# Feed-forward of an int4 layer: VectorE's down units moved to units 0, 4, 16 and 20, GpSimd's products and ScalarE's conversions re-placed

## The reference

```python
H = 1024; I = 3584; G = 128
Wg, Wu, Wd = (q.reshape(O, In // G, G) * s[:, :, None] for each of gate, up, down)   # q: int32 in [-8, 7]
xn = _layernorm(x)
gate_score = silu(xn @ Wg.T)
intermediate = gate_score * (xn @ Wu.T)
x = x + attention(xn) + intermediate @ Wd.T
```

## Time and profile before

| | |
|---|---|
| median of 3 runs | 2119.39 us |
| the profiled execution: its own time, its span | 2121.04 us, 2119.1 us |
| granted TensorE clock, mean | 0.993 |
| busy: PE, DVE, ACT, POOL | 95%, 75%, 59%, 64% |
| feed-forward | from about 855 us to the end |
| one tile of its loop | 42.79 us |

### The profile page before, as it was taken

How to read it: one execution, slowest core, us unless ns; L and a number is a source line. 1 busy time by engine, 2 the same in 40 slices (tenths; PEclk the granted TensorE clock), 3 DMA queues, 4 the chain that set the end, 5 groups by cost and what they waited for, 6 DMA issues and landing times. The chain is left out here.

```text
span 2119.1 us, 36938 instructions
## 1 busy us (share of the span) xinstructions
PE 2021.6 (95%) x10880; PEld 973.3 (46%) x10880; DVE 1589.2 (75%) x1584; ACT 1253.2 (59%) x2017; POOL 1348.6 (64%) x769
## 2 busy tenths in 40 slices
PE   7899999999998899989999999999999999999997
PEld 5555555555554444334444444444444444444444
DVE  5666766766765310399989998999899989999896
ACT  4577777777776321236565656565666566656653
POOL 1444554554554000048888888888888888888886
PEclk9999999999999999999999999999999999999998
DMA  8464454454455334122211221222112212222108
GB/s 284 94 130 89 94 125 98 89 124 104 89 116 141 112 112 173 30 53 67 59 47 47 69 59 45 49 69 59 45 49 69 57 47 49 54 64 55 49 21 322
DMA packets 330007, 185.97 MB, mean 88 GB/s; under 512 B 269169, under 2 KB 306033, under 8 KB 329969
## 3 DMA queue, kind: packets, MB, share of 16 engines
q1 hardware_dynamic: 329968, 185.46, 33.8%
HBM read 96.29 MB, written 25.17 MB: 57 GB/s over the span
## 5 line engine op out<-in xcount | busy, mean ns | idle before, releaser
L644 PE MATMUL banks<-xt,lower 128*128 128x512 f16 x3584 | 861.7, 379 | 29.8 <-ACT lower L895 16.1
L1212 POOL TENSOR_TENSOR acc<-acc,lower 128x1024 f32<-128x1024 f32 x327 | 771.5, 2364 | 176.4 <-ACT lower L922 176.3
L922 ACT ACTIVATE lower<-banks,down_scale 128x512 f32<-128x512 f32 x654 | 413.1, 682 | 356.6 <-PE banks L669 265.3
L1099 DVE SCALAR_TENSOR_TENSOR lower<-banks,gate_scale,lower 128x1024 f32<-128x1024 f32 x392 | 479.2, 1278 | 146.2 <-PE banks L644 140.3
L644 PEld LDWEIGHTS banks<-xt,lower 128*128 128x128 f16 x3584 | 337.3, 98 | 486.6 <-DVE lower L1099 80.3
L499 PE MATMUL banks<-wt,xt_tile 128*128 128x512 f16 x2304 | 542.0, 380 | 4.2 <-ACT wt L743 2.6
L1099 DVE SCALAR_TENSOR_TENSOR lower<-banks,up_scale,lower 128x1024 f32<-128x1024 f32 x392 | 479.5, 1278 | 50.9 <-PE banks L644 44.8
L669 PE MATMUL banks<-lower 128*128 (+1 forms) x1792 | 459.7, 381 | 4.6 <-DMA lower<-lower 4.4
L1174 POOL TENSOR_TENSOR stacks<-unit,stacks 128x512 f16<-128x512 f32 x192 | 246.9, 1306 | 303.7 <-ACT stacks L768 303.7
L499 PEld LDWEIGHTS banks<-wt,xt_tile 128*128 (+1 forms) x2304 | 215.2, 98 | 216.7 <-issue 4.2
L669 PEld LDWEIGHTS banks<-lower 128*128 (+1 forms) x1792 | 175.6, 98 | 217.7 <-issue 18.3
(11 more groups left out here) (57 smaller groups left out, 1320.3 us busy)
## 6 DMA issues: line engine op xcount, KB each, us to landing
lower<-in_L_ffn_gate_q_dram SPq DMA_DIRECT2D x28, 512.0 KB, 3.7
lower<-in_L_ffn_up_q_dram SPq DMA_DIRECT2D x28, 512.0 KB, 4.4
lower<-in_L_ffn_down_q_dram SPq DMA_DIRECT2D x28, 512.0 KB, 4.0
x_tile<-in_L_attn_x_dram SPq DMA_DIRECT2D x16, 512.0 KB, 3.7
xt_scratch<-xt_tile SPq DMA_DIRECT2D x16, 512.0 KB, 2.8
ctx_scratch<-ctx_parts SPq DMA_DIRECT2D x64, 128.0 KB, 2.1
lower<-ctx_scratch SPq DMA_DIRECT2D x4, 2048.0 KB, 9.0
xt<-xt_scratch SPq DMA_DIRECT2D x4, 2048.0 KB, 15.5
```

What stands on the lines that cost most here:

```text
L644: last = mm(psum[:, 2 * (slot % 3) + c, :], gu_t[:, mat, g, :], xt[:, (2 * half + c) * CT:(2 * half + c + 1) * CT, part, g, :], start=(par ...
L922: run(down_tmp[:, buffer, c * BANK:(c + 1) * BANK], psum[:, 6 + c, :], ACT.Copy, scale=scale)\
L1099: v.scalar_tensor_tensor(out=acc_of[:, half, :], in0=gu_pair(slot % 3), scalar=scale[:, :, :].rearrange("p t k -> p (t k)")[:, bass.ds(t * ...
L1212: g.tensor_tensor(acc[:, half, ho, :], acc[:, half, ho, :], down_tmp[:, buffer, :], ALU.add).then_inc(down_added, 1)
```

## The change

VectorE's four down units become d8 and d10 (behind units 0 and 4) and d0 and d2 (behind units 16 and 20); `slow_rank` and `SLOTS` follow. GpSimd's product of the second half moves from `idx` 10 to 16 and its LO part from 18 to 21; ScalarE's HI part of it from 13 to 20, the second `silu` from 23 to 27. The gate weights are converted at 9 instead of 21, the up weights at 29 instead of 27, and the down weights at 25 of their own tile, not at 7 of the next; SyncE's order of loads and transposes follows.

```diff
         def by_dve(d):
-            return d % 4 == 0
+            return d % 8 in (0, 2)
 
         def slow_rank(d):
-            return d - d // 4 - 1
+            return sum(not by_dve(e) for e in range(d))
...
-            if unit % 8 == 0:
+            if unit % 16 in (0, 4):
                 SLOTS.append(("down", unit))
...
-        CONV_DOWN, CONV_GATE, CONV_UP = 7, 21, 27
-        HI_AT0, HI_AT1 = 3, 13
-
-        POOL_AT = {0: ("h", 0), 4: ("l", 0), 10: ("h", 1), 18: ("l", 1)}
+        CONV_GATE, CONV_DOWN, CONV_UP = 9, 25, 29
+        HI_AT0, HI_AT1 = 3, 20
+        SILU_AT = {19: 0, 27: 1}
+
+        POOL_AT = {0: ("h", 0), 4: ("l", 0), 16: ("h", 1), 21: ("l", 1)}
...
-                    if idx == CONV_DOWN and has_prev(t):
-                        conv(DOWN, t - 1)
+                    if idx == CONV_DOWN:
+                        conv(DOWN, t)
                     if idx in (HI_AT0, HI_AT1) and has_prev(t):
                         hidden_hi(t - 1, int(idx == HI_AT1))
-                    if idx in (19, 23):
-                        silu(t, (idx - 19) // 4)
+                    if idx in SILU_AT:
+                        silu(t, SILU_AT[idx])
...
             tiles(act, tile)
-            conv(DOWN, NI - 1)
             hidden_hi(NI - 1, 0)
             hidden_hi(NI - 1, 1)
...
-                    sp.wait_ge(gu_done, units_made(t, DOWN_SLOT[8]))
+                    sp.wait_ge(gu_done, units_made(t, DOWN_SLOT[4]))
...
             def tile(t):
                 load_q(GATE, t + 1)
                 load_q(UP, t + 1)
-                if has_prev(t):
-                    turn_q(DOWN, t - 1)
-                    load_q(DOWN, t)
                 turn_q(GATE, t + 1)
+                turn_q(DOWN, t)
+                load_q(DOWN, t + 1)
                 turn_q(UP, t + 1)
...
-            turn_q(DOWN, NI - 2)
-            load_q(DOWN, NI - 1)
             turn_q(DOWN, NI - 1)
```

## The result

The changed kernel takes 2124.99 us, the median of 10 runs (2122.89 to 2125.76), beside 2119.36 us for the kernel before in the same rounds (10 runs, 2118.18 to 2121.11). The ratio is 1.0022, with a 95% interval of 1.0013 to 1.0030: slower by 0.22%, just past what can be told from no change.

The account below looks back on a forecast made before the run. TensorE was taken as the bound, only its late starts counting. Per tile -0.78 - 0.24 + 1.28 = +0.26, over 26 tiles +6.8, tail -2.2, sum +4.6: median 2124.0 us, profiled execution 2125.6, range 2118.5 to 2131.5.

Parts of the forecast that it names:

- The main step: Up half: unit 17's first group waits for GpSimd's product behind d15's add, so unit 20 starts 1.28 us late per tile.
- The old delay: Unit 18's late start, from ScalarE waiting for GpSimd's product before its HI part, goes: gain 0.78 us a tile.
- VectorE's 0.24: Late start behind VectorE's down units: moves from unit 10 to 6 in the gate half, vanishes in the up half.
- the rival of a second delay at unit 22: VectorE's add of unit 20 ends too late, so its 0.24 stays: +6.2 us, 2130.2 us; chance 14%.
- The tile's sum: Loop tile: -0.78 - 0.24 + 1.28 = +0.26 us, over 26 tiles +6.8 us.
- The tail's term: The 4.41 us wait for the last down weights goes, TensorE stands again before d11: gain 2.2 us, between 1.2 and 2.9.
- the clock's: Tail: if the clock falls to half rate behind the stand, d12 to d14 take twice 0.86, about 1.3 us lost.
- The fast rival: GpSimd's product ends before 5.6 us after d15's start, so unit 20 is on time: 2096.9 us; chance 10%.
- The rival of the tail giving all its 7.2 us: In the tail, wait and half clock both go, 7.2 us instead of 2.2: 2119.0 us; chance 10%.
- The weighed rule: VectorE and GpSimd lock shared ports when VectorE's instruction has two SBUF inputs; down units, one input in PSUM, are free.

Follow-up runs that it names:

- Experiment 1: The changed kernel with GpSimd's product of the second half at position 12 instead of 16, ahead of d15's add: 2097.38 us, ratio to before 0.9889.
- experiment 4: The changed kernel with GpSimd's second product on 512 of 1024 columns in tiles 0 to 26, the rest left out: 2096.66 us, ratio 0.9887.
- Experiment 5: The kernel before with ScalarE's second-half HI part moved from 13 to 20 (LO part to 21, second silu to 27), product still at 10: 2097.66 us.
- experiment 2: The kernel before with only VectorE's four down units moved, to 0, 4, 16 and 20: 2119.19 us, ratio 0.9996.
- experiment 3: The kernel before with only the conversions moved (gate 9, down 25 of their own tile, up 29) and SyncE's order of the change: 2118.54 us.
- experiment 7: The changed kernel with d9's and d11's tail copies earlier and VectorE's adds of d8 and d10 ahead of its second product and LO parts: 2124.64 us.
- experiment 6: The changed kernel with ScalarE's tail copy of d9 ahead of both HI parts and that of d11 between them: 2129.16 us, ratio to before 1.0042.
- experiment 9: The changed kernel with d9's and d11's tail copies earlier and GpSimd's adds of both on 64 of 1024 columns: 2121.66 us, ratio 1.0006.
- experiment 8: The changed kernel with the product at 12, earlier d9 and d11 tail copies, and VectorE's d8 and d10 adds ahead of its second product: 2097.68 us.

## Why the prediction was right, and where its terms were off

**The main step held as it was written.** The place (unit 20), the releaser (unit 17's first group), what that waits for (GpSimd's product behind d15's add) and each link were read off the other half of the tile: 2.22, 4.53, 6.89, 7.04, 8.22 forecast, 2.23, 4.53, 6.90, 7.02, 8.19 measured, and a delay of 1.29 for 1.28. Experiment 1 removes the delay by the order alone; experiment 4 takes 1.09 of it by the length of the product alone.

**The old delay went** for the reason given: ScalarE waited at 13. Experiment 5 shows it without the rest of the change (0.80 a tile, for 0.78); experiment 2 shows the placing of VectorE's units with the delay still there. Nobody behind the waiting first group was late either. One sum on the way is off: ScalarE's three jobs there add up to 3.4, not 3.2; measured, they end 11.18 after d15's start, and nothing hangs on it.

**VectorE's 0.24.** In the gate half it moved to unit 6, in the up half it was absorbed, as forecast; the rival of a second delay at unit 22 did not come. With the delay at unit 20 gone it came back (experiment 1: a tile of 41.93, where 42.97 - 1.29 + 0.24 gives 41.92).

**The tile's sum was 0.26, measured 0.18.** The missing 0.08: before the change the units behind d8 and d0 start 0.89 us after the down unit (1358.27 to 1359.16), now 0.86 and 0.87, which is 0.05 to 0.06 in the tile; 0.02 more is unit 18's 0.80, which the sum took at 0.78. The small pauses belong to the units' placing: experiment 2 has 0.86 too, experiments 3 and 5, with the units where they were, still 0.89. What makes them was not settled. 26 tiles: +6.8 forecast, +4.9 measured.

**The tail's term was mis-sized: -2.2 forecast, -0.6 measured.** Where TensorE stands and for what was right (before d11, for ScalarE's copy behind the HI parts). One price was wrong, the clock's: it stayed down for 13 matmuls from d11 on, 5.41 us by the window instead of 2.8. That is 2.6 lost, where I took 1.3, and only as a possibility. So d14's copy came at 2078.57, and GpSimd's chain of adds, which was to run on from d11's, had to wait for it:

```profile
2079.92 2.37 POOL L1212 TENSOR_TENSOR acc<-acc,lower 128x1024 f32<-128x1024 f32 x1 [1.08 <-ACT lower L923]
```

GpSimd's adds of d9 and d11 (2073.19) ran 5.65 us for two where I had 2.36 each, and VectorE's second LO part 2.17 us. Neither cost anything here: GpSimd was done 1.08 us before d14's add could start, and TensorE ran on without a pause. How long the clock stays down is not fixed by the stand: behind the same stand of 3.86 us the 64 matmuls took 15.82 us in experiments 3 and 4. There the tail gives up to 1.5, still not the 2.2.

The two misses, 1.9 in the loop and 1.6 in the tail, cancel, which is luck: the changed stretches give +4.3 for +4.6. These 4.3 lie inside the interval of the measured +5.6 (2.8 to 6.4 us); the other 1.3 are not placed.

**The fast rival** (the product early enough) failed by the 1.28 us of chain at which it was said to decide. Experiment 4 takes away all but 0.20 of them and reaches 2096.7, near the rival's 2096.9. That the two are so close is partly luck: the rival had a tile of 42.01 and 2.2 from the tail, the measured ones are 41.93 and 0.1 to 1.5. The rival of the tail giving all its 7.2 us didn't come: with the wait for the weights gone, ScalarE's order made the next.

**The weighed rule** on VectorE and GpSimd held in both directions. VectorE's down units, with one input in PSUM, take 1.28 beside GpSimd's product as before (L1121, 1279 ns on the mean after, 1280 before). Its operations with two inputs in SBUF take 1.2 us when they start with GpSimd idle (or just ahead of its add, experiment 7) and 2.2 to 3.4 when they start under a running add (experiments 6, 7 and 9). The Trainium skill, page SBUF — State Buffer, section "SBUF: two separate sides", has it so: the two lock a shared pair of ports against each other for a whole operation. I used it for the loop and did not ask what it does to the tail.

## What to carry to other kernels

When a step moves later in one engine's queue, look for every instruction that waits for it, the overwriting ones too: the next tile's first write of the same buffer may stand right behind the new place. The chain can be measured in the trace of before wherever the same sequence occurs at another place, and it then holds to a few hundredths. A change of several parts that looks neutral can hold a gain and a loss of the same size: here one position (12 for 16) turns 0.22% slower into 1.1% faster. In a tail, letting one engine start earlier is no gain when it then holds up another: GpSimd's adds from 2071.39 on made the end 58.8 us instead of 55.9 (experiment 6).

## What the runs showed of the hardware

**The stretch before the change differs by up to 5 us between executions; TensorE's clock in it differs too.** The windows of the first stage, of the kernel before and of the changed one, whose code there is the same:

```profile
0.00:30.00 30.00, 19.63 (x99) 14.82 (x100) 13.47 (x15) 10.86 (x12) 3.07 (x9) 0.89 0.90 305
50.00:70.00 20.00, 16.32 (x92) 10.45 (x90) 13.28 (x17) 10.17 (x13) 5.53 (x4) 0.91 0.53 128
680.00:700.00 20.00, 14.22 (x88) 7.84 (x88) 5.10 (x7) 10.46 (x24) 2.26 (x2) 0.91 0.54 197
```

```profile
0.00:30.00 30.00, 17.79 (x99) 13.18 (x100) 13.37 (x15) 10.91 (x12) 3.05 (x9) 0.94 0.89 303
50.00:70.00 20.00, 16.31 (x99) 10.22 (x98) 13.47 (x17) 11.10 (x15) 5.67 (x5) 1.00 0.59 140
680.00:700.00 20.00, 14.32 (x84) 7.76 (x85) 5.81 (x7) 9.78 (x23) 2.26 (x2) 0.91 0.45 164
```

The mean granted clock is 0.89, 0.91 and 0.91 in these windows before and 0.94, 1.00 and 0.91 in the changed kernel; in experiment 8 it is 0.89, 0.91 and 0.83. Tile 2's first group starts at 952.60, 950.21 and 954.89, and at 949.97 in experiment 5. The clock falls to its lower level (1.2 GHz) for a different share of the same work. It is not what sets the time, or not alone: experiments 1 and 2 have the three clocks of experiment 8 and start tile 2 at 952.13 and 952.57, and experiment 3 has 0.94, 1.00 and 0.83 and starts it at 953.01. What moves the stretch stays open. A profiled execution is therefore compared stretch by stretch, and a difference of 2 us in the whole says nothing about the changed part.

**TensorE's clock behind a stand.** In the changed kernel TensorE stood 3.87 us by the bracket, and the next 13 matmuls ran at half clock. In experiment 9 it stood 2.95 us, and the granted clock of the 6 us from 2073 on was 1.00. The time at the lower level differs from execution to execution: the mean clock of the 6 us behind the same stand is 0.52 in experiment 1 (3.87 us, from 2047.4) and 0.72 in experiments 3 and 4 (3.86 us, from 2070.3 and 2047.0).

**GpSimd's add beside VectorE's two-input operations is stretched too**: 2.36 us alone, 3.06 and 3.17 in experiment 6 (6.34 for the two with the pause between them), up to 3.40 in experiment 7.
